# A chunked delta-rule attention on one core: the query left unnormalized, its squares added to the output's, the carried decay moved ahead of a product, and one masking in place of two

## The reference, cut to what matters

```python
q = rmsnorm(q) * HD ** -0.5;  k = rmsnorm(k) * HD ** -0.5      # eps 1e-6, over the 128 features of a head
q = q * HD ** -0.5
g = cumsum(g within a chunk);  decay = where(tril, exp(g_i - g_j), 0)
T = inverse(eye + strict_lower((k * beta) @ k.T * decay))
v_c = T @ (v * beta);  k_cumdecay = T @ (k * beta * exp(g))
for each chunk:                                   # state: 128 x 128 for each head
    v_new = v_c - k_cumdecay @ state
    out   = (q * exp(g)) @ state + (q @ k.T * decay) @ v_new
    state = state * exp(g_last) + (k * exp(g_last - g)).T @ v_new
h = norm_w * rmsnorm(out) * silu(z)               # eps 1e-6, over the 128 features of a head
x = x + layernorm(h @ W_out.T)                    # then a mixture of 34 experts on x
```

## Time and profile before

| | |
|---|---|
| median of 3 runs (lowest to highest) | 1482.04 us (1478.9 to 1484.2) |
| profiled execution: its time, its span | 1480.87 us, 1479.0 us |
| PE, DVE, ACT, POOL busy | 89%, 77%, 68%, 35% of the span |
| mean granted clock of TensorE | 0.974 of full speed |

### The profile page before, as it was taken

One profiled execution on the slowest core, in us unless ns is written; L12 is line 12 of the kernel. 1 busy time (PEld: TensorE's weight loads), 2 busy tenths in 40 slices (PEclk: granted clock), 3 DMA queues, 4 the chain that ended last, 5 costly groups with the idle time before them and its releaser, 6 DMA issues.

```text
span 1479.0 us, 34092 instructions
## 1 busy us (share of the span) xinstructions
PE 1309.4 (89%) x11516; PEld 927.9 (63%) x11516; DVE 1138.0 (77%) x2414; ACT 1002.5 (68%) x2170; POOL 517.4 (35%) x599
## 2 busy tenths in 40 slices
PE   2679999999999999999999999999987559999995
PEld 2247666766667676767667676766665436666664
DVE  4678978889898989888898989898866445555555
ACT  2579788897979798888979797988865212222221
POOL 0134242334334242433333342424323105555550
PEclk9999999999999999999999999999999859999998
DMA  2111010101011010101010110100001016444441
GB/s 82 41 39 52 9 51 9 52 9 58 14 47 44 16 52 9 51 9 52 9 58 27 33 45 16 52 23 16 23 15 33 1 36 182 150 150 152 157 153 39
DMA packets 44659, 76.37 MB, mean 52 GB/s; under 512 B 7172, under 2 KB 26022, under 8 KB 44488
## 3 DMA queue, kind: packets, MB, share of 16 engines
q1 hardware_dynamic: 44488, 74.19, 16.1%
HBM read 72.85 MB, written 1.32 MB: 50 GB/s over the span
## 4 chain that ended last, share of the span: by engine, by line
PE 70%; DVE 16%; issue 7%; ACT 5%; DMA 1%; DVEq 1%; SPq 1%; ACTq 0%
PE bank L563 13%; PE bank L517 9%; PE bank L780 8%; PE bank L733 6%; DVE sil L1132 5%; PE bank L710 5%; PE bank L606 4%; PE bank L724 3%; PE bank L618 3%; PE bank L582 3%; PE bank L646 2%; PE bank L638 2%; DVE t L1192 2%; PE bank L713 2%; PE bank L696 2%
## 5 line engine op out<-in xcount | busy, mean ns | idle before, releaser
L563 PE MATMUL bank<-xT,whl 128*128 128x512 f16 x1152 | 298.3, 383 | 18.1 <-DVE sil L1132 8.3
L1132 DVE SCALAR_TENSOR_TENSOR sil<-bank,cw,sil 128x510 f32<-128x510 f32 (+2 forms) x384 | 283.3, 738 | 7.1 <-ACT sil L855 4.5
L1393 POOL TENSOR_TENSOR nl<-nt,n 128x512 f16<-128x512 f32 x64 | 74.1, 1157 | 523.6 <-ACT n L939 523.6
L1192 DVE CAST_PREDICATED t<-levm,bank 128x256 f16<-128x256 uint8 x384 | 166.1, 433 | 90.4 <-PE bank L638 74.5
L1021 ACT ACTIVATE kq<-vtok 128x512 f16<-128x512 f32 x94 | 59.2, 630 | 192.1 <-DVE vtok L1323 192.1
L950 ACT ACTIVATE x<-bank 128x256 f16<-128x256 f32 x320 | 125.6, 393 | 69.7 <-PE bank L618 68.2
L1205 DVE CAST_PREDICATED u<-levm,bank 128x256 f16<-128x256 uint8 x384 | 162.9, 424 | 0.2
L1323 DVE SCALAR_TENSOR_TENSOR vtok<-bank,b1s,zs 128x512 f32<-128x512 f32 x94 | 70.6, 751 | 117.6 <-PE bank L517 117.6
L563 PEld LDWEIGHTS bank<-xT,whl 128*128 128x128 f16 x1152 | 97.2, 98 | 94.9 <-DVE sil L1132 12.7
L618 PEld LDWEIGHTS bank<-t,n 128*128 128x128 f16 x1536 | 84.4, 98 | 89.2 <-DVE t L1192 59.8
L517 PE MATMUL bank<-xT,wmhl 128*128 128x512 f16 x564 | 139.2, 384 | 0.0
(11 more groups left out here) (156 smaller groups left out, 3118.1 us busy)
## 6 DMA issues: line engine op xcount, KB each, us to landing
grow<-rowsc SPq DMA_DIRECT2D x64, 256.0 KB, 3.3
wt<-wqkvz SPq DMA_DIRECT2D x16, 768.0 KB, 4.5
wms<-wm SPq DMA_DIRECT2D x47, 256.0 KB, 4.0
...
```

Source lines behind the costliest of these rows:

```text
L563: mm = nc.tensor.matmul(dst[:, :], whl[:, h, k, col:col + HD], xT[:, l, k, half * 512:(half + 1) * 512], start=(k == 0 and m == 0), stop=( ...
L1132: nc.vector.scalar_tensor_tensor(out=dst[:, :, late:S], in0=src[:, :, 0:S - late], scalar=cw[:, q, i, 3 - late:4 - late], in1=dst[:, :, la ...
L1192: nc.vector.copy_predicated(halves(t16[:, pair(U)], n)[:, :, :, 0], by4(2 * n, n), packed(X_BANK, n)).then_inc(s_tup, 1)
```

## The change

- The query is no longer normalized. `silu` of q writes straight into `kq`; the fills 14 and 15, their evictions, the second `norm` on ACT and on DVE and the second `square` are gone, and a group has 18 fills. Since a row of the output scales with its query's norm, the output's own norm absorbs it, except for the epsilon: for this the squares of q (`square_q`, one POOL instruction of 128x1024 for each group) are added to the scaled squares of the output for each unit (`square_sum`, POOL, 128x512, in place in `hsq`), and `ss` waits for that instead of for `squares`.
- `carried_part` now also scales the keys' cross block with the carried decay: two POOL instructions of 128x256 for each unit in place of one. `p` waits for them, is two matmuls of 128 columns in place of one of 256, and leaves its sum open in PSUM; `y1` of chunk 1 adds to it. `right_side` is one DVE subtraction of 128x256 in place of four instructions of 128x128, and `r1` is gone.
- The two product banks are one PSUM tensor, and `mask` is one DVE instruction of 128x512 in place of two of 128x256. It waits for all of `kk`.
- `SLOT` and `FRONT` are written anew. On PE `o` now stands between `w6` and the next `w0`; `t0` stands at the end of the slot before on DVE; `sqr` stands early in a slot rather than at the end of the one before; `nl` moved to the following slot.
- Tensors of the experts' layer (`lg`, `lrep`, `gates`, `gT`) lie in `sil`.

```diff
-FILLS = 20
+FILLS = 18
...
-SLOT = [("w", 0, 0), ("ln", 0, 2), ("xe", 1, 0), ("front", 0, 0), ("u", 6, 1), ("front", 1, 0), ("rex", 0, 2),
-        ("front", 2, 0), ("at", 1, 0), ("front", 3, 0), ("v0s", 0, 1), ("vn", 0, 1), ("y0", 0, 1), ("front", 4, 0),
-        ("xe", 2, 0), ("ss", 0, 2), ("t", 0, 0), ("x", 1, 0), ("u", 0, 0), ("y1", 0, 1), ("front", 5, 0),
-        ...
-        ("front", 33, 0), ("xe", 6, 0), ("front", 34, 0), ("n16", 0, -1), ("front", 35, 0), ("sqr", 0, 1),
-        ("front", 36, 0), ("x", 6, 0), ("o", 0, 1), ("w", 6, 0), ("front", 37, 0), ("g", 0, 0), ("front", 38, 0)]
+SLOT = [("w", 0, 0), ("front", 0, 0), ("sqr", 0, 2), ("front", 1, 0), ("exb", 0, 0), ("front", 2, 0), ("u", 0, 0),
+        ("xe", 1, 0), ("front", 3, 0), ("y0", 0, 1), ("front", 4, 0), ("t", 1, 0), ("front", 5, 0), ("g", 0, 1),
+        ("front", 6, 0), ("x", 1, 0), ("front", 7, 0), ("u", 1, 0), ("front", 8, 0), ("w", 1, 0), ("ss", 0, 2),
+        ...
+        ("p", 0, 1), ("u", 2, 0), ("x", 4, 0), ("front", 16, 0), ("proj", 0, 2), ("cap", 0, -1), ("front", 17, 0),
+        ("ht", 0, 2), ("t", 3, 0), ("front", 18, 0), ("at", 1, 1), ("front", 19, 0), ("qx", 0, 0), ("u", 3, 0),
+        ("vn", 0, 1), ("front", 20, 0), ("xe", 4, 0), ("y0", 1, 1), ("qx", 1, 0), ("front", 21, 0), ("r1h", 0, 1),
+        ("front", 22, 0), ("nl", 0, 0), ("front", 23, 0), ("w", 4, 0), ("front", 24, 0), ("eye", 1, -1),
+        ...
+        ("t", 0, -1), ("xe", 6, 0), ("front", 36, 0), ("hsum", 0, 1), ("front", 37, 0), ("vn", 1, 1), ("at", 0, 0),
+        ("front", 38, 0), ("w", 6, 0), ("o", 0, 1), ("front", 39, 0), ("n16", 0, -1)]
...
             def y1_(U, c):
-                else:
-                    wait_u(pe, s_r1, U, 2, 2)
-                nc.tensor.matmul(R_BANK[:, 0:256], eye[:, 0], guess, start=True, stop=False, skip_group_check=True)
+                nc.tensor.matmul(R_BANK[:, 0:256], eye[:, 0], guess, start=(c == 0), stop=False, skip_group_check=True)
...
             def p(U, _):
-                wait_u(pe, s_cross, U, 1, 1)
+                wait_u(pe, s_qx, U, 2, 2)
                 wait_u(pe, s_v0s, U, 2, 2)
                 wait_u(pe, s_r, U, 2, 1)
-                nc.tensor.matmul(R_BANK[:, 0:256], cross[:, pair(U), 0], v0s[:, pair(U)].rearrange("p v d -> p (v d)"),
-                                 start=True, stop=True).then_inc(s_p, 1)
+                for v in range(2):
+                    mm = nc.tensor.matmul(R_BANK[:, v * P:(v + 1) * P], qx[:, third(U), v, 0], v0s[:, pair(U), v],
+                                          start=(v == 0), stop=False, skip_group_check=True)
+                mm.then_inc(s_p, 1)
...
             def ss(U, _):
-                wait_u(pe, s_hsq, U, 1, 1)
+                wait_u(pe, s_hsum, U, 1, 1)
...
-                nc.scalar.activation(hsq[:, pair(U)], KQ_BANK[:, :], ACT.Square).then_inc(s_hsq, 1)
+                nc.scalar.activation(hsq[:, pair(U)], KQ_BANK[:, :], ACT.Square, scale=EPS_RMS ** -0.5 / HD).then_inc(s_hsq, 1)
...
-            def mask(U, c):
-                wait_u(dve, s_kk, U, 2, c + 1)
-                nc.vector.tensor_tensor(kqm[:, w, c], src, mask2, ALU.mult).then_inc(s_mask, 1)
+            def mask(U, _):
+                wait_u(dve, s_kk, U, 2, 2)
+                nc.vector.tensor_tensor(kqm[:, w], products[:, :].rearrange("p (c k h i) -> p c k h i", c=2, k=2, h=2)[:, :, :, 0],
+                                        mask2.unsqueeze(1).to_broadcast([P, 2, 2, P]), ALU.mult).then_inc(s_mask, 1)
...
-            def right_side(U, dst, ready):
-                for v in range(2):
-                    nc.vector.scalar_tensor_tensor(
-                        out=dst[:, v], in0=R_BANK[:, v * P:(v + 1) * P],
-                        scalar=sc[:, q, C_NEG, v, 2 * b + 1:2 * b + 2],
-                        in1=vtok[:, q, 2 * b + 1, v], op0=ALU.mult, op1=ALU.add).then_inc(ready, 1)
+            def right_side(U, _):
+                nc.vector.tensor_tensor(r1h[:], vtok[:, q, 2 * b + 1],
+                                        R_BANK[:, 0:256].rearrange("p (v d) -> p v d", v=2), ALU.subtract
+                                        ).then_inc(s_r1h, 1)
...
+            def square_sum(U, _):
+                (G, b), q = U, U[0][1] % 2
+                wait_g(pool, s_qsq, G, 1, 1)
+                wait_u(pool, s_hsq, U, 1, 1)
+                h = hsq[:, pair(U)].rearrange("p (v s) -> p v s", v=2)
+                nc.gpsimd.tensor_tensor(h, h, qsq[:, q, b * S:(b + 1) * S].unsqueeze(1).to_broadcast([P, 2, S]), ALU.add
+                                        ).then_inc(s_hsum, 1)
...
-            def carried_part(U, _):
-                nc.gpsimd.tensor_tensor(qx[:, third(U)], cross[:, w, 1:2].to_broadcast([P, 2, P]), exb[:, w], ALU.mult
-                                        ).then_inc(s_qx, 1)
+            def carried_part(U, v):
+                nc.gpsimd.tensor_tensor(qx[:, third(U), v], cross[:, w], exb[:, w, v].unsqueeze(1).to_broadcast([P, 2, P]),
+                                        ALU.mult).then_inc(s_qx, 1)
```

More of the change, by code:

```diff
@@ new lines @@
+FRONT = {
+    (0, 2): [("fill", 1, 1)],
+    (0, 3): [("evict", 1, 1)],
+    (0, 4): [("tap", 2, 1)],
+    (0, 6): [("cw", 0, 2)],
+    (0, 8): [("rest", 1, 1), ("tap", 3, 1)],
+    (0, 12): [("fill", 2, 1)],
+    (0, 13): [("rest", 2, 1)],
+    (0, 21): [("tap", 4, 1)],
+    (0, 22): [("tap", 5, 1)],
+    (0, 27): [("evict", 2, 1), ("tap", 6, 1)],
+    (0, 28): [("fill", 3, 1)],
+    (0, 33): [("tap", 7, 1)],
+    (0, 34): [("tap", 8, 1), ("rest", 3, 1)],
+    (1, 0): [("evict", 3, 1)],
+    (1, 1): [("fill", 4, 1)],
+    (1, 2): [("tap", 9, 1)],
+    (1, 3): [("tap", 10, 1)],
+    (1, 4): [("evict", 4, 1)],
+    (1, 8): [("rest", 4, 1)],
+    (1, 13): [("fill", 5, 1), ("tap", 11, 1)],
+    (1, 15): [("rest", 5, 1)],
+    (1, 19): [("tap", 12, 1)],
+    (1, 20): [("evict", 5, 1), ("tap", 13, 1)],
+    (1, 24): [("tap", 14, 1)],
+    (1, 27): [("tap", 15, 1), ("silu", 0, 1)],
+    (1, 30): [("fill", 6, 1)],
+    (1, 31): [("tap", 16, 1)],
+    (1, 32): [("tap", 17, 1)],
+    (1, 34): [("tap", 18, 1), ("rest", 6, 1)],
+    (1, 36): [("tap", 19, 1)],
+    (1, 38): [("evict", 6, 1)],
+    (2, 4): [("tap", 20, 1), ("fill", 7, 1)],
+    (2, 5): [("evict", 7, 1), ("tap", 21, 1)],
+    (2, 7): [("tap", 22, 1)],
+    (2, 8): [("rest", 7, 1)],
+    (2, 9): [("fill", 8, 1), ("rest", 8, 1)],
+    (2, 11): [("tap", 23, 1), ("evict", 8, 1)],
+    (2, 12): [("fill", 9, 1)],
+    (2, 13): [("rest", 9, 1), ("fill", 10, 1)],
+    (2, 15): [("silu", 1, 1), ("rest", 10, 1)],
+    (2, 18): [("sc", 0, 1), ("silu", 2, 1)],
+    (2, 20): [("evict", 9, 1)],
+    (2, 22): [("fill", 11, 1), ("rest", 11, 1)],
+    (2, 23): [("evict", 10, 1)],
+    (2, 25): [("silu", 3, 1)],
+    (2, 27): [("evict", 11, 1), ("fill", 14, 1)],
+    (2, 35): [("fill", 12, 1)],
+    (2, 36): [("sq", 0, 1)],
+    (3, 0): [("fill", 13, 1), ("evict", 14, 1), ("evict", 12, 1)],
+    (3, 3): [("evict", 13, 1), ("wo", 0, 1)],
+    (3, 5): [("hi", 0, 1)],
+    (3, 8): [("fill", 15, 1)],
+    (3, 10): [("evict", 15, 1)],
+    (3, 11): [("fill", 16, 1)],
+    (3, 12): [("owts", 0, 1)],
+    (3, 13): [("weights", 1, 1), ("lo", 0, 1)],
+    (3, 14): [("fill", 17, 1)],
+    (3, 16): [("nexp", 0, 1)],
+    (3, 17): [("qsq", 0, 1)],
+    (3, 23): [("nmul", 0, 1)],
+    (3, 26): [("hi", 1, 1)],
+    (3, 27): [("fill", 0, 2), ("evict", 16, 1)],
+    (3, 28): [("lo", 1, 1)],
+    (3, 29): [("evict", 17, 1)],
+    (3, 34): [("tap", 0, 2)],
+    (3, 37): [("rest", 0, 2), ("tap", 1, 2)],
+    (3, 39): [("evict", 0, 2)],
@@ L1407, in carried_part @@
                 wait_u(pool, s_o, (G, b - 3), 1, 1)
-                nc.gpsimd.tensor_tensor(qx[:, third(U)], cross[:, w, 1:2].to_broadcast([P, 2, P]), exb[:, w], ALU.mult
-                                        ).then_inc(s_qx, 1)
-            attention({"cw": scale_cw, "wo": scale_wo, "sq": square, "eye": start_inverse, "nl": low_n,
+                nc.gpsimd.tensor_tensor(qx[:, third(U), v], cross[:, w], exb[:, w, v].unsqueeze(1).to_broadcast([P, 2, P]),
+                                        ALU.mult).then_inc(s_qx, 1)
+            attention({"cw": scale_cw, "wo": scale_wo, "sq": square, "qsq": square_q, "hsum": square_sum, "eye": start_inverse, "nl": low_n,
                        "at": attention_part, "qx": carried_part})
```

235 lines of the change are left out of this document (79 added, 156 removed), and 5 rows, old and new, of the table SLOT.

## The result

The changed kernel takes 1459.6 us (median of 4 runs, 1456.2 to 1462.2), the kernel before 1483.1 on the same chip: a ratio of 0.985, 95% interval 0.982 to 0.987. That is 1.5% faster, inside the range of 1410 to 1475 us; 23 us were gained where 42 were forecast. The time lies above the forecast's own 1424 to 1456 us and in the 1457 to 1477 us of rival 1.

The account below looks back on a forecast made before the run. Three engines near their limit, TensorE at 94%, were taken to bound a group; terms of -1.8, -1.2, -0.5, +0.3 and +0.6 us gave -2.6 a group, -41.6 for 16, hence 1440 us, range 1410 to 1475.

Parts of the forecast that it names:

- rival 1: Only TensorE's relief counts, VectorE's is eaten by meetings with POOL: 1457 to 1477 us, chance 0.22.
- PE's 62.0 us of busy time: Sign that the prediction is right: TensorE busy for about 62.0 us of a group, from 63.8 before.
- the 65.3 us of a group: Sign that the prediction is right: a group of four units takes 65.3 us in place of 67.9.
- the longest slot, shorter by 1.5 to 2 us: Sign that the prediction is right: a group's longest stretch, read as 19.2 us, shrinks by 1.5 to 2 us.
- TensorE, -1.8 us a group: Query norm's fills 14 and 15 gone from TensorE: 1.78 us a group, counted in full.
- VectorE, -1.2 us: Right side, masking and query norm take 4.3 us less on VectorE a group; half of a usable 2.3 counted.
- `w0`, -0.5 us (down to -2.0): `o` between `w6` and `w0` fills TensorE's 2.0 us of waits a group; a quarter counted.
- The path to `ss`, +0.3 us: POOL's addition ahead of `ss` expected mostly hidden: +0.3 us a group, between 0 and +5.2.
- rival 3: TensorE stands at `ss` waiting for POOL's late `square_sum`, 1.3 us in each unit: slower, 1522 us, chance 0.10.
- Meetings of VectorE and GpSimd, +0.6 us: VectorE's `hT` slowed by POOL's instructions at the same time: +0.6 us a group, between nothing and 2.4.
- Rival 4: No change, as the inverse's round trips set the slot and VectorE's waits for `w` grow: 1478 to 1486 us, chance 0.05.

Follow-up runs that it names:

- the cuts: Low half of the projections' weights left out, 5.1 us a group less TensorE work: changed kernel 1443.1 us against 1459.6 uncut, kernel before 1477.0 against 1482.8.
- both cuts: Third late convolution tap cut to 8 of 256 tokens, less VectorE work: changed kernel 1454.8 us, kernel before 1480.0 (uncut 1482.8 on its chip).

## Why the prediction was right, and where it was not

The time is inside the range and the sign is right, and the terms behind it are mostly not; that they still added up to a time in the range is in part luck. Of the signs that were named, PE's 62.0 us of busy time (64.0), the 65.3 us of a group and the longest slot, shorter by 1.5 to 2 us, did not come: it went from 18.56 to 17.28 us, but its neighbour grew from 16.85 to 17.89.

- **TensorE, -1.8 us a group.** The work fell as worked out (55.9 to 54.2 us of columns). "I count all of it" is the step that failed: by the cuts, a microsecond of the projections' matmuls is worth 0.1 to 0.2. For the query's own fills no kernel here gives the price by itself; the one with the query's part alone shows 0.5 us of the 1.8 outside the trip with `ss`, and leaves the rest open.
- **VectorE, -1.2 us.** The instructions came out as worked out: 0.41 for the right side, 0.68 for the masking. DVE's busy time fell by 3.3 us in place of 4.3, since the meetings with POOL gave 1.2 back. The price of the relief was half in the forecast and nothing in both cuts, and less than nothing for the right side in the old order. The reading of the earlier trace rows was the error: 94% busy in a stretch was taken for a bound. In the changed kernel 147 of the 349 `t` between 140 and 1100 us waited for their data; the others and every `u` but the last of a unit started right behind the instruction ahead of them, so VectorE's order is in the chain at some places and its load at none that the tap's cut touched.
- **`w0`, -0.5 us (down to -2.0).** The wait is gone completely, but it was 0.8 us for a group and not 2.0: the prediction added the waits of PE and PEld for the same matmuls, and the earlier trace rows put PEld's part down to "issue". The price came out near the term for another reason: the two trips next to `o` are 0.9 us shorter, with either steps. Other steps moved there as well, and no kernel here undid `o`'s place alone.
- **The path to `ss`, +0.3 us.** Hidden but for 0.17 us once in a group, and without the addition the group is as long. The mechanism of rival 3 is real: 1.1 us of waiting and 1.3 us of length in a unit, once the order of before is kept, half of the wait by my placing. By the timeline it was the place of `sqr`, right at the start of a slot, and of what stands ahead of `ss` on PE that kept it away; no kernel moved these alone.
- **Meetings of VectorE and GpSimd, +0.6 us.** They happen as expected (0.865 us for `hT` on average, median 0.85), and where they hit `hT` they cost about 0.3 us for a group: right in mechanism, half in size. A meeting of another instruction ahead of a `t` cost 1.0 us. The Trainium skill's rule (page "SBUF — State Buffer", section "SBUF: two separate sides") describes them: VectorE with two SBUF inputs and GpSimd take turns. The rows agree in both directions, `hT` 1.04 us behind `nl` and the copy 1.09 in place of 0.61 behind `hT`; in size they stay a little under a full block (`hT` 0.36 us longer where `nl` had 0.48 us left). Blocking is time in the engine's record; whether it is time of the kernel depends on what stands behind it.
- **Rival 1**, PE alone, has the measured time in its range, and not by its mechanism: it counts 1.8 us of PE's relief in full.
- **Rival 4**, which I gave 0.05, was nearest to the cause, with the wrong time. The round trips with the steps in them do set the slots, at a length that the order changes, and DVE's waits for `w`, its sign, grew once `t0`'s are counted with them (the row of 61.8 us alone fell to 47.9). It left out that they had room to gain in the slots above 15.6 us: together these stood 5.2 us above it before (18.56 + 16.50 + 15.67 + 16.85 - 4 x 15.6) and 4.0 after.

What remains unsettled is which single move of the new order carries the 1.2 us; 0.9 of it lies in the two trips next to `o`. What is shown is that the steps need the order and the order, with the places that I gave the old steps, needs them, that the taps' load on VectorE has no part in the length, and that GpSimd's has one only through meetings ahead of a `t`. How short a slot could get is argued from the trips' pieces; no kernel here shortened one of them.
